# Cross-attention and routed experts on one core: a third pair of stacks, four stored copies for both batches, a loop body of six steps

## The chip, the cores and the metric

One NeuronCore of a Trainium2 chip runs the whole program; the other cores are idle. The metric is the device time of one launch in microseconds (us), less is better. Engines are named as in the profile: PE (TensorE), DVE (VectorE), ACT (ScalarE), POOL (GpSimd), SP (SyncE, which only issues DMAs). A name with q, such as SPq, is the engine's sequencer.

## The reference, cut to what matters

```python
# x, ctx: (128 batches, 128 tokens, 256)
q = layernorm(x) @ Wq.T;  k = ctx @ Wk.T;  v = ctx @ Wv.T
# q, k: 32 sub-heads of 8 dims; v: 16 heads of 16 dims
att = softmax(q @ k.T / sqrt(8))               # per sub-head, 128 x 128
att = att[:, :, 0] - lam * att[:, :, 1]        # pairs of sub-heads
x = x + att @ v
h = layernorm(x)
top2 of sigmoid(h @ gate_w.T) over 16 experts, weights normed, times 2.5
x = x + sum over the 2 experts of w_e * (silu(h @ w_gate_e) * (h @ w_up_e)) @ w_down_e
      + (silu(h @ ws_gate) * (h @ ws_up)) @ ws_down
```

## The kernel before

**Steps.** The 128 batches go in pairs: 64 attention steps, each with two batches (u = 0, 1) of 128 tokens. Every engine runs the same software pipeline: while step `it` has its scores, softmax and output made (stage c), step it+1 (stage b) has its values and its row maxima made, step it+3 (stage a) its projections, it-1 and it-2 the second layer norm and the routing. After the steps, 144 tiles of 128 gathered rows go through the experts.

**Stacks.** The scores of a sub-head have only 8 contraction dims. So q and k are split into three bf16 parts each, and six products of parts (q0k0, q1k1, q2k0, q0k1, q1k0, q0k2) are stacked along the contraction dim: 48 rows. Two halves h of 16 sub-heads each sit at partitions 0 and 64. To get from tokens of features into this layout, the parts are written to `stack_dram` (`put_parts`, L349) and read back as rows (`load_stacks`, L358) into `q_st` and `k_st`, two bf16 tiles of 8 KB a partition for each of two parities. Before, each of the six copies of each operand is written once: 12 DMAs of 128 KB a step, and 8 DMAs of 192 KB read them back, one for each of q and k, u and h.

**Maxima.** `maxima` (L490) multiplies the first 48 rows to get the scores by query, DVE reduces them (`reduce_max`, L982), PE turns the maxima (L543), ACT copies them (`copy_max`, L798) and SP writes them as two more rows of `q_st` (`put_max`, L365), so that `scores` (L483, 50 rows) gives scores less the row's maximum. Slot k of a step's 16 has 4 score matmuls and 4 matmuls of maxima of the next step; `both` (L497) holds their waits: `d_stk` at k = 0, 4, 8, 12 for the maxima's stacks, `d_m` at k = 0 and 8 for the maxima's rows of the scores.

**SP's order.** SP's `step` (L384) is written out by hand: what stands behind a waiting DMA waits too. The two halves u of a stack are loaded at different times, since with two parities a buffer comes free by halves.

**Loop.** `steps` (L308) gives each engine steps -4 to 3 as straight code, then a hardware loop (`Fori`, L302) whose body is two steps, run 27 times, then steps 58 to 66 as straight code. In the loop, waits compare with a register (L282, L294).

Of the kernel before, what the change touches and what calls it, by code (L numbers as in the profile page):

```python
# [22 lines left out]
P = 128  # L23
# [3 lines left out]
COPIES = 6  # L27
Q_COPIES, K_COPIES = (0, 1, 2, 0, 1, 0), (0, 1, 0, 1, 0, 2)
# [15 lines left out]
class Step:  # L44
# [11 lines left out]
    def par(self):  # L56
        return self.off % 2

# [9 lines left out]
def program(nc, x, ctxT, lq1, lk1, lq2, lk2, wqT, wkT, wvT, gate_wT, w_gu, w_dn, ws_gu, ws_dn, out):  # L68
# [25 lines left out]
    stack_dram = nc.dram_tensor("stack_dram", (2, 2, 2, 2, COPIES, HALF, SHH, P), BF16, kind="Internal").ap()  # L94
# [5 lines left out]
    with ExitStack() as st:  # L100
# [34 lines left out]
        def stack(n):  # L135
            return stacks.bitcast(BF16)[:, n * SHH * SW:(n + 1) * SHH * SW].rearrange("p (u j t) -> p u j t", u=2, j=SHH)

        q_st, k_st = [stack(0), stack(2)], [stack(1), stack(3)]
# [85 lines left out]
        d_stk = [[sem(f"d_stk{u}{h}") for h in range(2)] for u in range(2)]  # L224
# [36 lines left out]
        STK = 2 * 16  # L261
# [8 lines left out]
        first, lo, hi, end = -4, 4, NS - 6, NS + 3  # L270
        PAD_STEPS = (*range(lo), *range(hi, hi + 4))
# [36 lines left out]
        def steps(eng, body):  # L308
            pipeline(eng, body, first, lo, hi, end, 2)
# [28 lines left out]
        def _(sp):  # L338
# [10 lines left out]
            def put_parts(s, n, part, landed, copies, at):  # L349

                for u in range(2):
                    for h in range(2):
                        wait(sp, d_stk[u][h], STK, s, -STK)
                for i in at:
                    sp.dma_start(stack_dram[s.par(), n, :, :, i].rearrange("h u d j t -> (d j) (h u) t"),
                                 part[:, copies[i], :].rearrange("p (v t) -> p v t", t=P)).then_inc(landed, 16)

            def load_stacks(s, u, h):  # L358

                p = s.par()  # L360
                for n, buf in ((0, q_st[p]), (1, k_st[p])):
                    sp.dma_start(buf[64 * h:64 * h + ROWS, u, :, :].rearrange("p j t -> p (j t)"),
                                 stack_dram[p, n, h, u].rearrange("r d j t -> (r d) (j t)")).then_inc(d_stk[u][h], 16)

            def put_max(s, u):  # L365

                wait(sp, a_mT, 2, s, u + 1)
                for h in range(2):
                    row = 64 * h + ROWS
                    sp.dma_start(q_st[s.par()][row:row + 2, u, :, :],  # L370
                                 mxT[u][2 * SHH * h:2 * SHH * (h + 1), :]).then_inc(d_m[u], 16)
# [12 lines left out]
            def step(it):  # L384
# [6 lines left out]
                if b.is_in(0, NS):  # L391
                    wait(sp, p_st, NCH, it)
                    wait(sp, p_mx, NCH, b)
                    load_stacks(b, 1, 1)
                    load_stacks(b, 1, 0)
                if n2.is_in(0, NS):
                    wait(sp, g_qs, 1, n2, 1)
                    put_parts(n2, 0, qp, d_qw, Q_COPIES, range(PARTS))
                if it.is_in(0, NS):
                    put_max(it, 1)  # L400
                if n2.is_in(0, NS):
                    put_parts(n2, 0, qp, d_qw, Q_COPIES, range(PARTS, COPIES))
                    wait(sp, g_ks, 1, n2, 1)
                    put_parts(n2, 1, kp, d_kw, K_COPIES, range(COPIES))
# [4 lines left out]
                if n2.is_in(0, NS):  # L409
                    wait(sp, p_st, NCH, it, NCH // 2)  # L410
                    wait(sp, p_mx, NCH, b, NCH // 2)
                    wait(sp, d_qw, PW_Q, n2, PW_Q)
                    wait(sp, d_kw, PW_K, n2, PW_K)
                    if n2.k is None and n2.off < 2:
                        sp.wait_ge(g_ones, n2.off + 1)
                    load_stacks(n2, 0, 1)
                if b.is_in(0, NS):
                    put_max(b, 0)
                if n2.is_in(0, NS):
                    load_stacks(n2, 0, 0)  # L420
                if b.is_in(0, NS):
                    wait(sp, g_x2, 4, it, 0)
                    sp.dma_start(x_res[1 - p][:, :, :],
# [1045 lines left out]
```

## Time and profile before

| | |
|---|---|
| median of three timed runs | 2260.15 us (2256.93 to 2262.98) |
| the profiled execution, its own time | 2249.22 us |
| its span, first to last instruction | 2247.5 us |
| PE, DVE, ACT, POOL busy | 90%, 71%, 63%, 64% of the span |
| granted PE clock, mean | 0.972 |
| DMA packets | 616,921, of them 447,811 under 512 B |

The span divides into a start (0 to 65 us), 64 steps (65 to about 1675 us) and the experts' tiles. Busy shares are averages over these; what a change is worth must be read in the stretch that it touches, from what ends the waits there. PE rows have modelled ends, so a gap of PE is to be read from the starts of its groups.

### The profile page before, as it was taken

What the parts mean: (1) busy time and instruction counts of PE and PEld (TensorE: products, weight loads), DVE (VectorE), ACT (ScalarE), POOL (GpSimd) and SP (SyncE); (2) the same over time, 40 slices, a digit from 0 to 9 for tenths busy, and PEclk for the clock granted to TensorE, in tenths of its full rate; (3) what the DMA queues carried; (4) which work ended last, traced back from release to release, by engine and by line L of the source; (5) the groups of instructions that cost most, each with busy time, mean ns of one, the idle gap of its engine ahead of it and who ended that gap; (6) DMA issues with size and microseconds to landing.
All of it is one profiled execution on the core that took longest, in us unless ns stands there. A gap on an engine that the chain in (4) does not pass through costs nothing.

```text
span 2247.5 us, 76469 instructions
## 1 busy us (share of the span) xinstructions
PE 2021.7 (90%) x20840; PEld 1405.2 (63%) x20840; DVE 1584.5 (71%) x4623; ACT 1426.2 (63%) x3511; POOL 1446.2 (64%) x2183
## 2 busy tenths in 40 slices
PE   4999999999999999999999999999977988889996
PEld 3666665566656566656656566666546877768775
DVE  3777777777777777778777777778765655546554
ACT  2777777777777777777776777777763444434443
POOL 4466777767677676767676767767664555545554
PEclk8899999999999999999999999999987999999999
DMA  5997777777777777777777777878846777667774
GB/s 133 222 225 192 187 195 190 178 189 184 191 190 184 186 194 185 185 183 182 191 193 178 184 188 190 194 181 216 228 173 180 223 214 214 199 178 220 220 223 127
DMA packets 616921, 432.05 MB, mean 192 GB/s; under 512 B 447811, under 2 KB 562634, under 8 KB 616400
## 3 DMA queue, kind: packets, MB, share of 16 engines
q1 hardware_dynamic: 556528, 319.91, 58.3%
q0 software_dynamic: 32256, 84.47, 11.8%
q10 hardware_dynamic: 28000, 26.03, 3.8%
q8 instruction: 64, 1.05, 0.2%
q14 instruction: 73, 0.60, 0.1%
HBM read 234.59 MB, written 197.72 MB: 192 GB/s over the span
## 4 chain that ended last, share of the span: by engine, by line
PE 67%; DVE 15%; issue 10%; ACT 3%; DMA 2%; SPq 1%; POOL 1%; DVEq 1%; another core or an unknown queue 1%; ACTq 0%; POOLq 0%
PE mx_ps L494 11%; PE o_ps L527 7%; DVE mx L982 6%; PE ms_ps L778 5%; PE o_ps L538 5%; PE ms_ps L555 5%; PE mx_ps L557 4%; PE mx_ps L555 4%; PE ms_ps L576 4%; PE st_ps L756 3%; PE mx_ps L556 3%; PE ms_ps L583 3%; PE st_ps L487 3%; PE ms_ps L556 3%; PE ms_ps L557 2%
## 5 line engine op out<-in xcount | busy, mean ns | idle before, releaser
L982 DVE TENSOR_REDUCE mx<-mx_ps 128x4 f32<-128x512 f32 x1024 | 686.3, 685 | 300.4 <-PE mx_ps L494 294.2
L826 ACT ACTIVATE prob<-st_ps 128x512 f32<-128x512 f32 x1024 | 604.5, 598 | 357.8 <-PE st_ps L487 353.5
L494 PE MATMUL mx_ps<-stacks 48*128 48x128 bf16 x4096 | 396.7, 221 | 67.6 <-DVE mx L982 33.8
L487 PE MATMUL st_ps<-stacks 50*128 50x128 bf16 x4096 | 394.9, 220 | 0.0
L494 PEld LDWEIGHTS mx_ps<-stacks 48*128 48x128 bf16 x4096 | 230.9, 95 | 228.6 <-issue 105.9
L527 PE MATMUL o_ps<-prob,v_sb 128*32 128x256 f32 x4096 | 331.6, 396 | 0.8 <-ACT prob L826 0.4
L1344 POOL DMA_INDIRECT rows_dram<-rowt,posi x256 | 253.7, 991 | 67.6 <-issue 64.3
L555 PE MATMUL ms_ps<-e_lo 128*128 128x256 f32 x768 | 264.7, 345 | 18.1 <-issue 11.1
L923 ACT ACTIVATE rows_T<-st_ps 128x256 fp32r<-128x256 f32 x288 | 111.7, 388 | 192.2 <-PE st_ps L756 137.3
L487 PEld LDWEIGHTS st_ps<-stacks 50*128 50x128 bf16 x4096 | 229.8, 95 | 2.5 <-issue 1.5
L1413 POOL DMA_INDIRECT sums_dram<-stacks x144 | 141.7, 984 | 130.4 <-DVE stacks L1220 70.2
L1417 POOL DMA_INDIRECT out<-stacks x144 | 141.7, 984 | 121.7 <-issue 62.6
L556 PE MATMUL ms_ps<-e_lo 128*128 128x256 f32 x768 | 219.7, 286 | 0.0
L557 PE MATMUL ms_ps<-e_lo 128*128 128x256 f32 x768 | 219.2, 285 | 0.0
L555 PE MATMUL mx_ps<-e_hi,rows_T 128*128 x576 | 192.3, 334 | 27.7 <-DVE prob L1213 25.6
L555 PEld LDWEIGHTS ms_ps<-e_lo 128*128 128x128 f32 x768 | 147.6, 192 | 97.2 <-issue 69.9
L1207 DVE TENSOR_TENSOR rows_lo<-st_ps,rows_T 128x256 fp32r<-128x256 f32 x288 | 121.1, 421 | 95.5 <-issue 51.1
L1220 DVE SCALAR_TENSOR_TENSOR stacks<-ms_ps,stacks 128x256 f32<-128x256 f32 x288 | 138.6, 481 | 67.2 <-PE ms_ps L778 49.0
L778 PE MATMUL ms_ps<-w_dn_sb,v_sb 128*128 x576 | 176.3, 388 | 1.0 <-DVE stacks L1220 0.4
L1350 POOL DMA_INDIRECT base_dram<-base_t,posi x128 | 139.1, 1087 | 53.1 <-issue 47.9
L538 PE MATMUL o_ps<-ident,oT 128*128 128x128 f32 x1024 | 169.6, 289 | 0.4 <-issue 0.4
L557 PE MATMUL mx_ps<-e_hi,rows_lo 128*128 x576 | 165.0, 286 | 0.0
(155 smaller groups left out, 4694.4 us busy)
## 6 DMA issues: line engine op xcount, KB each, us to landing
stack_dram<-w_dn_sb SPq DMA_DIRECT2D x768, 128.0 KB
stacks<-stack_dram SPq DMA_DIRECT2D x512, 192.0 KB
stacks<-rows_dram SPq DMA_DIRECT2D x288, 130.0 KB
w_dn_sb<-in_x SPq DMA_DIRECT2D x64, 256.0 KB
w_dn_sb<-in_ctxT SPq DMA_DIRECT2D x64, 256.0 KB
x_res<-in_x SPq DMA_DIRECT2D x64, 256.0 KB
stacks<-sums_dram SPq DMA_DIRECT2D x78, 128.0 KB
stacks<-base_dram SPq DMA_DIRECT2D x76, 128.0 KB
```

The lines of the kernel that those rows point to most:

```text
L487: return pe.matmul(st_ps[k % 2][:, i * P:(i + 1) * P], k_st[p][64 * h:64 * h + KROWS, u, j, :], q_st[p][64 * h:64 * h + KROWS, u, j, :], s ...
L494: return pe.matmul(mx_ps[k % 2][:, i * P:(i + 1) * P], q_st[p][64 * h:64 * h + ROWS, u, j, :], k_st[p][64 * h:64 * h + ROWS, u, j, :], sta ...
L527: mm = pe.matmul(OT[SLOT * g:SLOT * (g + 1), gg * SW:(gg + 1) * SW], v_sb[s.par()][:, (u * HEADS + 2 * c + i) * SLOT:(u * HEADS + 2 * c + ...
L538: mm = pe.transpose(out_ps, src, ident[:, :])
L555: pe.matmul(out_ps, rnd(still[0]), rnd(moving[0]), start=start, stop=False)
L556: pe.matmul(out_ps, rnd(still[0]), rnd(moving[1]), start=False, stop=False)
L557: return pe.matmul(out_ps, rnd(still[1]), rnd(moving[0]), start=False, stop=stop)
L778: pe.matmul(eo_ps[t.off % 2][:, 0:D], hid_T[t.off % 4][:, :], w_dn_sb[:, bass.ds(down, 1), :].rearrange("p e n -> p (e n)"), start=True, s ...
L826: nc.scalar.activation(prob[k % 4][:, :], st_ps[k % 2][:, :], ACT.Exp, scale=float(HALF) ** -0.5).then_inc(a_exp, 1)
L982: v.tensor_reduce(mx[:, u, c * CHUNK:(c + 1) * CHUNK], mx_ps[k % 2][:, :].rearrange("p (c n) -> p c n", c=CHUNK), AX.X, ALU.max).then_inc( ...
L1344: g.indirect_dma_start(rows_dram[k][:, :], bass.IndirectOffsetOnAxis(ap=posi[p][:, u, k:k + 1], axis=0), rowt[p][:, u, :], None).then_inc( ...
L1413: g.indirect_dma_start(sums_dram[:, :], bass.IndirectOffsetOnAxis(ap=row[:, C_NEXT:C_NEXT + 1], axis=0), sums, None, bounds_check=N_FIRST ...
```

## The change

- `COPIES` goes from 6 to 4. `stack_dram` has one row for both batches (512 B runs instead of 256 B), and the parts are written with 8 DMAs of 128 KB a step instead of 12. The stored order is q parts (0, 1, 2, 0) and k parts (2, 0, 0, 1); the load reads all four and then two of them again (from copy 0 for q, from copy 2 for k), which gives the same six products.
- `load_stacks` brings both batches at once, with 8 DMAs: for q, then k, the 32 rows of four copies and the 16 rows of two, each for h = 1 and then h = 0. The tile's layout has u inside.
- A third pair of stacks lies in the last 16 KB a partition of `e_hi`, which nothing else uses until the last steps. A step's stack is its number modulo 3. POOL sets three key tiles to -1 at the start instead of two.
- The loop's body becomes six steps (2 and 3 both divide it), run 9 times.
- `d_stk` becomes one semaphore for each h and parity; PE waits for it at k = 0 and k = 4 only.
- SP's step: all loads of step it+2 come after its own puts and the context's load, then x's load, then the maxima's rows of step it+1 for u = 0, then the residual.

```diff
-COPIES = 6
-Q_COPIES, K_COPIES = (0, 1, 2, 0, 1, 0), (0, 1, 0, 1, 0, 2)
+COPIES = 4
+Q_COPIES, K_COPIES = (0, 1, 2, 0), (2, 0, 0, 1)
+Q_AGAIN, K_AGAIN = 0, 2
...
-    stack_dram = nc.dram_tensor("stack_dram", (2, 2, 2, 2, COPIES, HALF, SHH, P), BF16, kind="Internal").ap()
+    stack_dram = nc.dram_tensor("stack_dram", (2, 2, 2, COPIES, HALF, SHH, SW), BF16, kind="Internal").ap()
...
+        def stack_of_experts(n):
+            whole = e_hi[:, :, :, :].rearrange("p e k n -> p (e k n)").bitcast(BF16)
+            return whole[:, (2 + n) * SHH * SW:(3 + n) * SHH * SW].rearrange("p (j w) -> p j w", j=SHH)
+
+        q_st, k_st = [stack(2), stack_of_experts(0), stack(0)], [stack(3), stack_of_experts(1), stack(1)]
...
-            pipeline(eng, body, first, lo, hi, end, 2)
+            pipeline(eng, body, first, lo, hi, end, 6)
...
+            def load_stacks(s):
+
+                p, i = s.par(), s.third()
+                for n, buf, again in ((0, q_st[i], Q_AGAIN), (1, k_st[i], K_AGAIN)):
+                    for row, copy, m in ((0, 0, COPIES), (COPIES * HALF, again, 2)):
+                        for h in (1, 0):
+                            sp.dma_start(buf[64 * h + row:64 * h + row + m * HALF, :, :].rearrange("p j w -> p (j w)"),
+                                         stack_dram[p, n, h, copy:copy + m].rearrange("r d j w -> (r d) (j w)"),
+                                         max_dma_last_dim=4096).then_inc(d_stk[h][p], 16)
...
-                if b.is_in(0, NS):
-                    wait(sp, p_st, NCH, it)
-                    wait(sp, p_mx, NCH, b)
-                    load_stacks(b, 1, 1)
-                    load_stacks(b, 1, 0)
...
                 if n2.is_in(0, NS):
-                    wait(sp, p_st, NCH, it, NCH // 2)
-                    wait(sp, p_mx, NCH, b, NCH // 2)
+                    wait(sp, p_st, NCH, it)
+                    wait(sp, p_mx, NCH, it)
                     wait(sp, d_qw, PW_Q, n2, PW_Q)
                     wait(sp, d_kw, PW_K, n2, PW_K)
...
-                    load_stacks(n2, 0, 1)
...
+                    load_stacks(n2)
...
-                    if k % 4 == 0:
-                        wait(pe, d_stk[u][1 - k // 4 % 2], STK, b, STK)
+                    if k in (0, 4):
+                        wait_par(pe, d_stk[1 - k // 4], STK, b)
...
-            for i in range(2):
-                g.memset(k_st[i][:, :, :, :], -1.0).then_inc(g_ones, 1)
+            for i in range(3):
+                g.memset(k_st[i][:, :, :], -1.0).then_inc(g_ones, 1)
```

SP's DMAs in one whole step (step 3, the last ahead of the loop), before. `stack_dram<-w_dn_sb` are the puts of the parts, `stacks<-stack_dram` the loads, `stacks<-mxT1` and `stacks<-mxT0` the maxima's rows of u = 1 and u = 0.

```order
L362 DMA stacks<-stack_dram 48x2048 x4
L355 DMA stack_dram<-w_dn_sb 128x4x128 x3
L370 DMA stacks<-mxT1 2x16x128 x2
L355 DMA stack_dram<-w_dn_sb 128x4x128 x9
L407 DMA w_dn_sb<-in_ctxT 128x512
L362 DMA stacks<-stack_dram 48x2048 x2
L370 DMA stacks<-mxT0 2x16x128 x2
L362 DMA stacks<-stack_dram 48x2048 x2
L423 DMA x_res0<-in_x 128x2x256
L427 DMA w_dn_sb<-in_x 128x2x256
```

The same step now; `e_hi` is the third pair of stacks.

```order
L363 DMA stack_dram<-w_dn_sb 128x2x256 x4
L381 DMA stacks<-mxT1 2x16x128 x2
L363 DMA stack_dram<-w_dn_sb 128x2x256 x4
L412 DMA w_dn_sb<-in_ctxT 128x512
L372 DMA stacks<-stack_dram 32x2x2048 x2
L372 DMA stacks<-stack_dram 16x2x2048 x2
L372 DMA stacks<-stack_dram 32x2x2048 x2
L372 DMA stacks<-stack_dram 16x2x2048 x2
L424 DMA w_dn_sb<-in_x 128x2x256
L381 DMA e_hi<-mxT0 2x16x128 x2
L429 DMA x_res0<-in_x 128x2x256
```

The maxima's rows of u = 0 had two loads ahead of them since the puts; they now have eight and the load of x.

At the start, before: the first stacks, from the puts of step 0 to those of step 1.

```order
L355 DMA stack_dram<-w_dn_sb 128x4x128 x12
L407 DMA w_dn_sb<-in_ctxT 128x512
L362 DMA stacks<-stack_dram 48x2048 x4
L427 DMA w_dn_sb<-in_x 128x2x256
L362 DMA stacks<-stack_dram 48x2048 x4
```

And now:

```order
L363 DMA stack_dram<-w_dn_sb 128x2x256 x8
L412 DMA w_dn_sb<-in_ctxT 128x512
L372 DMA stacks<-stack_dram 32x2x2048 x2
L372 DMA stacks<-stack_dram 16x2x2048 x2
L372 DMA stacks<-stack_dram 32x2x2048 x2
L372 DMA stacks<-stack_dram 16x2x2048 x2
L424 DMA w_dn_sb<-in_x 128x2x256
```

The first maxima needed the first two of the loads; they now need the seventh of eight.

## Rows read from the trace of the kernel before

**Rows 1.** The page: span, busy time, DMA share in 40 slices.

```profile
span 2247.5 us, 76469 instructions
PE 2021.7 (90%) x20840; PEld 1405.2 (63%) x20840; DVE 1584.5 (71%) x4623; ACT 1426.2 (63%) x3511; POOL 1446.2 (64%) x2183
DMA  5997777777777777777777777878846777667774
```

**Rows 2.** Windows: two steps in the loop, two steps behind it (length, busy, clock, DMA).

```profile
1302.50:1353.20 50.70, 47.08 (x553) 30.60 (x552) 39.38 (x117) 36.93 (x84) 35.92 (x59) 1.00 0.75 188
1531.60:1580.90 49.30, 46.88 (x553) 30.68 (x552) 39.17 (x117) 37.33 (x84) 36.63 (x59) 1.00 0.96 241
```

**Rows 3.** Line 494, 158 to 1550 us: what PE's idle time there waited for.

```profile
  DVE mx L982: 105.5, 260
  issue: 104.5, 427
```

**Rows 4.** Line 302, the loop's end: PE's sequencer, ns min/median/max.

```profile
L302 PEldq COMPARE_BRANCH  x27: 76/208/243, 205.4 to 1530.3; - x27
```

**Rows 5.** DMA queue of PE's instructions, 100 to 204 us, then 210 to 1530 us.

```profile
q8 instruction: 10, 0.16, 0.7%
q8 instruction: 1, 0.02, 0.0%
```

**Rows 6.** DMA issues: the smallest load of the start (KB each, us to landing).

```profile
gw_sb<-in_gate_wT SPq DMA_DIRECT2D x1, 16.0 KB, 4.0
```

**Rows 7.** PE's timeline at a loop's end, the branch at 814.5 us.

```profile
815.15 0.66 PE L538 MATMUL o_ps<-ident,oT 128*128 128x128 f32 x4
815.74 0.23 PE L494 MATMUL mx_ps<-stacks 48*128 48x128 bf16 x1
```

**Rows 8.** Windows: a step at the lower clock, and the next one.

```profile
841.30:867.90 26.60, 24.90 (x277) 15.99 (x278) 19.77 (x59) 18.61 (x43) 17.90 (x30) 0.94 0.74 179
867.90:893.40 25.50, 23.60 (x277) 15.33 (x276) 19.71 (x58) 18.47 (x43) 17.97 (x30) 1.00 0.76 187
```

**Rows 9.** Timelines of the step from 765.1 to 790.56 us: POOL, SP, ACT, PE.

```profile
775.46 1.16 POOL L1313 TENSOR_TENSOR w_dn_sb<-k_rest,w_dn_sb 128x512 bf16<-128x512 f32 x1 [0.68 <-ACT w_dn_sb L849]
776.98 3.22 SPq L355 DMA_DIRECT2D stack_dram<-w_dn_sb  x6
780.57 0.36 SPq L407 DMA_DIRECT2D w_dn_sb<-in_ctxT  x1
782.07 0.80 SPq L362 DMA_DIRECT2D stacks<-stack_dram  x2
784.18 1.31 SPq L370 DMA_DIRECT2D stacks<-mxT  x2
783.84 0.26 ACT L798 ACTIVATE mxT<-o_ps 64x128 bf16<-64x128 bf16 x1
790.56 0.23 PE L494 MATMUL mx_ps<-stacks 48*128 48x128 bf16 x1
```

**Rows 10.** The chain of waits at the start (start us, us, what).

```profile
40.18 4.00 DMA stacks<-stack_dram
78.14 3.38 DMA stack_dram<-w_dn_sb
83.12 3.80 DMA stacks<-mxT
```

**Rows 11.** SP's DMA queue: 765.1 to 769.1, 763.5 to 765.1, 778.2 to 781.2 us.

```profile
q1 hardware_dynamic: 256, 0.78, 86.9%
q1 hardware_dynamic: 502, 0.49, 94.7%
q1 hardware_dynamic: 2588, 0.64, 96.7%
```

**Rows 12.** POOL's timeline at the start.

```profile
3.70 6.96 POOL L1261 MEMSET stacks<- 128x4096 bf16 x2
16.23 0.22 POOL L1283 TENSOR_SCALAR ve<-mv 128x2 f32<-128x2 f32 x1 [4.05 <-DVE mv L1013]
```

More of the change, by code:

```diff
@@ L57, in par, with third @@
         return self.off % 2
+    def third(self):
+        return self.off % 3
     def pair(self):
@@ L135, in stack @@
         def stack(n):
-            return stacks.bitcast(BF16)[:, n * SHH * SW:(n + 1) * SHH * SW].rearrange("p (u j t) -> p u j t", u=2, j=SHH)
-        q_st, k_st = [stack(0), stack(2)], [stack(1), stack(3)]
+            return stacks.bitcast(BF16)[:, n * SHH * SW:(n + 1) * SHH * SW].rearrange("p (j w) -> p j w", j=SHH)
+        def stack_of_experts(n):
+            whole = e_hi[:, :, :, :].rearrange("p e k n -> p (e k n)").bitcast(BF16)
+            return whole[:, (2 + n) * SHH * SW:(3 + n) * SHH * SW].rearrange("p (j w) -> p j w", j=SHH)
+        q_st, k_st = [stack(2), stack_of_experts(0), stack(0)], [stack(3), stack_of_experts(1), stack(1)]
         prob = [sb(f"prob{i}", [P, 512]) for i in range(4)]
@@ L223, in program @@
         d_qw, d_kw = sem("d_qw"), sem("d_kw")
-        d_stk = [[sem(f"d_stk{u}{h}") for h in range(2)] for u in range(2)]
+        d_stk = [[sem(f"d_stk{i}{h}") for i in range(2)] for h in range(2)]
         d_m = [sem(f"d_m{i}") for i in range(2)]
@@ L260, in program @@
         PW_Q, PW_K = COPIES * 16, COPIES * 16
-        STK = 2 * 16
+        STK = 4 * 16
         MR = 2 * 16
@@ L270, in program @@
         first, lo, hi, end = -4, 4, NS - 6, NS + 3
+        assert (hi - lo) % 6 == 0 and (NS - 1) % 3 == 0
         PAD_STEPS = (*range(lo), *range(hi, hi + 4))
@@ L347, in _, with put_parts @@
                 sp.dma_start(lam_in[:, n, :], src.partition_broadcast(P)).then_inc(d_w, 16)
[L349 to L363, printed above, removed]
+            def put_parts(s, n, part, landed, copies):
+                for h in range(2):
+                    wait_par(sp, d_stk[h], STK, s.plus(-2))
+                for i, r in enumerate(copies):
+                    sp.dma_start(stack_dram[s.par(), n, :, i].rearrange("h d j w -> (d j) h w"),
+                                 part[:, r, :].rearrange("p (h w) -> p h w", h=2)).then_inc(landed, 16)
+            def load_stacks(s):
[6 more added lines that the diff above has]
+                                         max_dma_last_dim=4096).then_inc(d_stk[h][p], 16)
             def put_max(s, u):
@@ L369, in put_max @@
                     row = 64 * h + ROWS
-                    sp.dma_start(q_st[s.par()][row:row + 2, u, :, :],
+                    sp.dma_start(q_st[s.third()][row:row + 2, :, u * P:(u + 1) * P],
                                  mxT[u][2 * SHH * h:2 * SHH * (h + 1), :]).then_inc(d_m[u], 16)
@@ L401, in step @@
                 if n2.is_in(0, NS):
-                    put_parts(n2, 0, qp, d_qw, Q_COPIES, range(PARTS, COPIES))
                     wait(sp, g_ks, 1, n2, 1)
-                    put_parts(n2, 1, kp, d_kw, K_COPIES, range(COPIES))
+                    put_parts(n2, 1, kp, d_kw, K_COPIES)
                 if xs.is_in(1, NS):
@@ L428, in step @@
                                  x_g[bass.ds(xs.plus(1).idx(), 1)].rearrange("g p u d -> (g p) u d")).then_inc(d_x, 16)
+                if b.is_in(0, NS):
+                    put_max(b, 0)
+                    wait(sp, g_x2, 4, it, 0)
+                    sp.dma_start(x_res[1 - p][:, :, :],
+                                 x_g[bass.ds(b.idx(), 1)].rearrange("g p u d -> (g p) u d")).then_inc(d_res[1 - p], 16)
             steps(sp, step)
```

24 lines of the change are left out of this document (8 added, 16 removed).

## The prediction

> **What bounds the kernel now.** I read the page first, then windows of whole steps, then what PE's idle time waited for, then SP's timeline against the deadline that PE sets, and last the chain of waits at the start.
>
> The page has PE busy for 90% of a span of 2247.5 us; DMA is busy too, at seven to nine tenths [rows 1]. So the first question is whether DMA bounds anything. In the loop it doesn't. Two steps in the loop take 50.7 us, 25.35 each, at a DMA share of 0.75; two whole steps behind the loop, with the same 553 matmuls, take 49.3 us, 24.65 each, at a DMA share of 0.96 [rows 2]. More DMA, shorter steps. And line 494, where PE waits for the stacks and for the maxima's rows, sat idle for DVE (105.5 us) and for issue (104.5 us), with no line for a DMA [rows 3]. A step in the loop is a chain of PE, DVE and ACT.
>
> At the start it is otherwise. The chain of waits goes through the puts (3.38 us to land), the loads (4.00 us) and the maxima's rows (3.80 us) [rows 10], in the slices where the DMA share is nine tenths [rows 1]. That holds for steps 0 to 2 only; then PE's own work is longer.
>
> **The change part by part.** The sum is made against the profiled execution, 2249.2 us; the median of the timed runs, 2260.15, is 10.9 above it, and I add that at the end.
>
> *Fewer loop ends.* The loop's branch is taken 26 times now and 8 times after. One costs PE's sequencer 0.208 us [rows 4]: 18 x 0.208 = 3.7, say -4 us.
>
> *A longer body.* This is the term that I expect to decide. In straight code PE fetches ten blocks of 16 KB in 104 us, some 2.4 a step of 25 us; in the loop, from 210 to 1530 us, it fetches one [rows 5]. A body of two steps, five blocks, is held and isn't fetched again. A body of six steps is some 15 blocks. No row shows what the engine does with that. If it isn't held, each of the 8 taken branches goes to code that must come first. Bounds: 0, if it is held; 4.0 us, what the 16 KB load takes from issue to landing [rows 6]. PE has work queued when it branches at 814.5: it starts the next step's first group at 815.74 [rows 7], so about 1.0 us is covered. I take the far end, 4.0 - 1.0 = 3.0 us, x 8 = +24 us, because the nearest rows for code not held are those in straight code, where each block is fetched as it is reached. ACT, DVE and POOL have bodies three times as long too, and stall beside PE, not behind it: they wait for PE a third of the time.
>
> The Trainium skill (Runtime: NRT & Kernel Launch, Instruction fetch mechanics) gives TensorE an instruction memory of 128 KiB and the others 32 KiB, filled in blocks of 16 KiB, and says that a taken branch out of it must wait for the fetch. Rows 5 agree with it as far as they go: 80 KB was held. By that rule a body of some 240 KB stalls at each branch.
>
> *The clock.* A step in which the granted clock fell to 0.94 on average (a stretch at 1.2 instead of 2.4 GHz) took 26.6 us, the next 25.5 [rows 8]. A stall of 3 us may bring that on. Bounds 0 and 8 times 1.1; half, +4 us.
>
> *The puts.* Before, 12 x 512 = 6,144 packets of 256 B a step, 17.9 ns each (3.0 us x 16 x 0.967 / 2,588) [rows 11], its third row: 6.9 us of all 16 DMA engines. After, 2,048 packets of 512 B. Their price isn't in the trace; it lies between 17.9 ns and the 48 ns of a 1 KB packet (1.6 x 16 x 0.947 / 502) [rows 11], its second row, so 2.3 to 6.1 us; middle 4.2, 2.7 us less a step. In the loop this is hidden already (rows 2), and worth nothing. It counts at the start.
>
> *The loads and the maxima's rows, in the loop.* PE needs both the maxima's rows and all of the next stack's h = 1 at the next step's first group, 790.56 in the step shown [rows 9]. Before, the parts of k are ready at 776.62, six puts are issued to 780.20, the loads 1.87 us behind them at 782.07, the maxima's rows from 784.18 to 785.49. After: four puts, to 779.13; loads from 781.0; eight at 0.43 us to 784.4; x's load, 0.4; the maxima's rows, ready on ACT at 784.1, from 784.8 to 786.1. As issued, only 0.6 us later. But they stand behind 1.57 MB of stacks and 0.26 MB of x in one queue. The rows give two rates: 0.78 MB in 4.0 us, 195 GB/s, for loads beside POOL's scatters, and 0.49 MB in 1.6 us, 306 GB/s, for x [rows 11]. Two loads (0.39 MB) landed in 4.00 us [rows 10], 2 us more than their transfer, so the last row lands at 781.0 + 2 + 1.83 / rate: 789.0 at the better rate, 1.6 us early, and 792.4 at the worse, 1.8 us late. The middle falls on the deadline. I take 0, since the loads of both halves now alternate and fewer put packets stand in the way; the bad end is 1.8 x 58 steps = 104 us.
>
> *At the start.* The same order sits on the chain. In steps 0 to 2: two puts less, -1.1 us; six loads and x ahead of the maxima's rows, +3.0 us of issue; 1.44 MB more ahead in the queue, of which 3.0 us of issue drain about half at 250 GB/s, +2.8 us; less 2.7 for the puts: +2.0, x 3 = 6. For the very first stack, two puts less, seven loads instead of two to wait for: -1.1 + 2.2, and 1.0 MB more less what the issue drains, +1.8: 3. Together +9 us. POOL's third tile costs 3.5 us (6.96 / 2) ahead of an idle time of 4.05 [rows 12]: nothing.
>
> *Where the waits that go were.* PE's waits at k = 8 and 12 had long been met. The third pair of stacks removes SP's wait for the middle of a step; with six puts still running then, it wasn't what was late.
>
> Sum: -4 + 24 + 4 + 0 + 9 = +33. 2249.2 + 33 = 2282 profiled, 2293 as a median.
>
> **The rivals.**
>
> *The maxima's rows come late in every step* (25%). For it: the deadline is met by about nothing at the middle rate. Against: x's packets ran at 306 GB/s in the same queue, and the puts that come ahead are fewer. At 1.0 us a step, 58 more: 2351. The Trainium skill (SBUF — State Buffer, Can I just issue two DMAs to hit both halves?) says that loads at partitions 0 and 64 in flight together gain only 6%, since one transfer's span picks its ports. By that rule the alternating halves bring nothing, and the time is this rival's; the 195 GB/s of rows 11, for loads of one half after the other, don't contradict it.
>
> *The long body costs nothing* (15%). If the body is held, or its head is fetched ahead, the 24 and the 4 go: +5, 2265.
>
> *The loop's steps come down to the pace of the steps behind it* (18%), the other side: faster. The mechanism would be PE's idle time ahead of line 494 in the loop: the queue is less full, SP is less often late, two of PE's register waits a step go. Price: 0.7 us x 54 = 38 us [rows 2], so 33 - 38 without the stalls' 28, -33: 2227. It decides the sign only from 0.6 us a step if the stalls come, 0.1 if not. Against: rows 2, where DMA was busier in the faster steps, and rows 3, where the idle time is DVE's and issue's, which keep all their register waits.
>
> **How the numbers follow.** The forecast has 42%, the others 25, 15 and 18. Its own range is 2268 to 2312: stalls of 1 to 4 us at each branch, 0 to 15 us at the start. The range for 8 in 10 leaves out half of the faster case below 2225, and the worse part of the late rows above 2360. About 0.3%, 7 us, is what a measurement can tell from no change. Faster by more: 0.18. Within: most of the free long body and a little of the forecast, 0.14. Slower: 0.68.
>
> **What would show it.** Right: PE's instruction queue has some 15 packets of 16 KB for each of 9 passes, some 130 more than now; PE is idle by 2 to 3 us ahead of the first group behind each of 8 branches, 152 us apart; other steps in the loop stay at 25.2 to 25.5 us; the start is about 9 us longer. The late rows would show as idle time of line 494's group for the DMA of the maxima's rows in most steps, and the chain of waits going through them. The free body: no instruction packets in the loop, or many but no idle time at the branches. I am wrong on the other side if steps inside the body come under 24.9 us.

## The result, and the profile after

The changed kernel takes 2472.82 us (median of 4 runs, 2455.72 to 2483.22), the kernel before 2258.93 us on the same chip (4 runs, 2256.93 to 2262.98): a ratio of 1.0937, 95% interval 1.0871 to 1.1003. It is slower, as forecast, by 214 us where +33 was forecast, and outside the range.

Two more measurements of it gave 1.0866 (1.0792 to 1.0939) and 1.0966 (1.0904 to 1.1029). The kernels of the experiments ran on four chips: on two of them the kernel before takes 2259 and 2249 us, on the other two 2062 us. Each is compared with the kernel before on its own chip, by ratio. The changed kernel itself was not run on a chip of the 2062 us kind.

The page of the changed kernel, for [rows 1], with the chain's shares and the two queues of instructions:

```profile
span 2481.4 us, 74118 instructions
PE 2101.6 (85%) x20840; PEld 1476.5 (60%) x20840; DVE 1590.1 (64%) x4623; ACT 1449.1 (58%) x3511; POOL 1451.3 (58%) x2184
PEclk7888989899999889989899899898998899999999
DMA  4765555566655556665556566555673676757674
q8 instruction: 201, 3.29, 0.6%
q14 instruction: 273, 2.24, 0.4%
PE 46%; DMA 20%; SPq 13%; issue 9%; POOL 4%; DVE 3%; ACT 2%; another core or an unknown queue 2%; ACTq 0%; POOLq 0%; DVEq 0%
```

PE's busy share fell from 90 to 85%, and DMA is busy for five or six tenths where it was seven: over the whole span nothing is full. The time is waiting, and a fifth of the chain that ended last goes through transfers.

Windows (length, PE, PEld, DVE, ACT, POOL busy, clock, DMA share, GB/s): the first steps of before and of after, then three steps of after in the loop, the third with a loop end. They answer to [rows 2] and [rows 8].

```profile
65.40:158.10 92.70, 88.80 (x1065) 57.71 (x1066) 70.91 (x184) 71.90 (x157) 51.34 (x88) 0.95 0.96 231
```

```profile
72.70:186.60 113.90, 93.64 (x1045) 60.95 (x1046) 70.17 (x181) 72.71 (x156) 53.06 (x90) 0.87 0.66 170
449.90:478.50 28.60, 25.00 (x273) 16.52 (x274) 18.94 (x57) 18.30 (x41) 17.21 (x29) 0.91 0.57 142
478.50:507.20 28.70, 26.08 (x277) 17.02 (x277) 19.89 (x59) 18.86 (x41) 17.09 (x28) 0.88 0.56 139
507.20:538.30 31.10, 23.76 (x277) 15.53 (x278) 19.67 (x58) 18.60 (x41) 20.52 (x33) 0.93 0.63 153
```

Where the 233.9 us between the two profiled spans went (a step runs here from its first exponential on ACT to the next step's):

| part | before | after | difference |
|---|---|---|---|
| up to the first step | 65.4 | 72.7 | +7.3 |
| steps 0 to 3 | 92.7 | 113.9 | +21.2 |
| steps 4 to 57, mean x 54 | 25.47 | 28.96 | +188.5 |
| steps 58 to 62, mean x 5 | 23.91 | 26.96 | +15.3 |
| rest | | | +1.6 |

So 225 of 234 us are in the 63 steps, spread over all of them, with more in the first four (5.3 us each, against 3.5 and 3.1). What PE waited for at line 496 (494 before), whole span, for [rows 3]:

```profile
  issue: 297.9, 422
  DMA stacks<-mxT: 154.8, 51
  DVE mx L984: 99.0, 260
  DMA e_hi<-mxT: 33.1, 11
```

The maxima's rows (`mxT`), which had no line in [rows 3], are named 62 times in 63 steps. SP's timeline of the step from 478.5 to 507.2 us (start, us, issues), then PE at its end and the chain of waits, for [rows 9]:

```profile
491.00 1.96 SPq L363 DMA_DIRECT2D stack_dram<-w_dn_sb  x4
493.82 0.35 SPq L412 DMA_DIRECT2D w_dn_sb<-in_ctxT  x1
494.67 4.11 SPq L372 DMA_DIRECT2D e_hi<-stack_dram  x8
499.12 0.40 SPq L424 DMA_DIRECT2D w_dn_sb<-in_x  x1
499.71 1.34 SPq L381 DMA_DIRECT2D stacks<-mxT  x2
506.78 0.21 PE L496 MATMUL mx_ps<-e_hi 48*128 48x128 bf16 x1 [1.75 <-DMA stacks<-mxT]
```

```profile
500.43 6.21 DMA stacks<-mxT
```

The second of the two transfers of 8 KB takes 6.21 us from its issue. In that time the queue is busy with loads. SP's queue over the load stretch of this step (packets, MB, share of 16 engines):

```profile
q1 hardware_dynamic: 653, 1.80, 92.0%
```

That is 1.80 MB in 9.0 us (495.1 to 504.1), 200 GB/s, of the loads and of the packets behind them. SP's queue alone keeps the 16 DMA engines 92.0% busy in this stretch: here, unlike over the whole step, they are all but full.

A picture of the usual step comes from the single packets of the trace. The maxima's rows are SP's only packets of 256 B now, the stacks' loads the only ones of 4 KB; of those there are 384 a step in both kernels, so what is new is that they come in one go. Medians over steps 6 to 55, in us from the step's start; the version is described in the next section where it isn't one of the two:

| version | rows issued | first packet | last packet | next step starts |
|---|---|---|---|---|
| before | 17.1 | 18.1 | 19.2 | 25.3 |
| after | 20.3 | 26.1 | 27.2 | 28.5 |
| after, third run | 20.2 | 25.9 | 26.9 | 28.2 |
| x behind the rows | 19.1 | 24.0 | 25.0 | 27.0 |
| rows in ACT's queue | 16.9 | 22.7 | 24.6 | 26.8 |
| one half at a time | 20.7 | 28.2 | 29.2 | 30.6 |
| more bytes, to DRAM | 22.9 | 26.3 | 27.2 | 28.8 |
| rows between the halves | 17.4 | 20.8 | 21.8 | 24.4 |
| the same, no loop | 16.1 | 17.9 | 19.2 | 24.3 |

In after the loads are first issued at 15.6, their first packet starts at 16.7 and the last ends at 25.6; the rows' packets end at 27.2, and 1.3 us later the next step begins (0.8 us to PE's first matmul, the rest to the exponential). Where the rows end by 22, the step no longer depends on them. The third run, the one with more bytes, and the one without a loop are from the chip where the kernel before takes 2249 us; the other four from the chips with 2062 us.

### The profile page after: what moved, and what is told of

The parts are those of the page before. It is cut to its first block, busy times and chain, and to the rows that moved or that the text cites. A ratio compares the mean times of both kernels' runs of the same rounds, so it can differ in the third digit from the quotient of the medians.

```text
span 2481.4 us, 74118 instructions
## 1 busy us (share of the span) xinstructions
PE 2101.6 (85%) x20840; PEld 1476.5 (60%) x20840; DVE 1590.1 (64%) x4623; ACT 1449.1 (58%) x3511; POOL 1451.3 (58%) x2184
## 4 chain that ended last, share of the span: by engine, by line
PE 46%; DMA 20%; SPq 13%; issue 9%; POOL 4%; DVE 3%; ACT 2%; another core or an unknown queue 2%; ACTq 0%; POOLq 0%; DVEq 0%
DMA stacks<-mxT 9%; SPq L372 8%; PE mx_ps L496 6%; PE o_ps L529 5%; PE ms_ps L780 5%; DMA e_hi<-mxT 4%; PE ms_ps L578 4%; PE mx_ps L559 3%; PE mx_ps L557 3%; PE ms_ps L557 3%; DMA stack_dram<-w_dn_sb 3%; PE st_ps L758 3%; PE mx_ps L558 3%; PE ms_ps L551 2%; PE ms_ps L585 2%
## 5 line engine op out<-in xcount | busy, mean ns | idle before, releaser
L984 DVE TENSOR_REDUCE mx<-mx_ps 128x4 f32<-128x512 f32 x1024 | 692.0, 686 | 529.5 <-PE mx_ps L496 423.3
L496 PE MATMUL mx_ps<-stacks 48*128 48x128 bf16 x2752 | 281.0, 230 | 179.1 <-issue 63.1
L529 PE MATMUL o_ps<-prob,v_sb 128*32 128x256 f32 x4096 | 351.4, 417 | 1.0 <-ACT prob L828 0.4
L496 PEld LDWEIGHTS mx_ps<-stacks 48*128 48x128 bf16 x2752 | 163.8, 98 | 292.1 <-issue 173.8
L557 PE MATMUL ms_ps<-e_lo 128*128 128x256 f32 x768 | 290.5, 378 | 19.5 <-issue 10.8
L1346 POOL DMA_INDIRECT rows_dram<-rowt,posi x256 | 253.7, 991 | 67.6 <-issue 65.4
L489 PE MATMUL st_ps<-stacks 50*128 50x128 bf16 x2752 | 279.8, 228 | 0.8 <-ACT prob L828 0.8
L558 PE MATMUL ms_ps<-e_lo 128*128 128x256 f32 x768 | 240.2, 313 | 0.0
L557 PEld LDWEIGHTS ms_ps<-e_lo 128*128 128x128 f32 x768 | 167.2, 218 | 121.6 <-issue 97.8
L559 PE MATMUL ms_ps<-e_lo 128*128 128x256 f32 x768 | 238.6, 311 | 0.0
L1285 POOL TENSOR_SCALAR ve<-mv 128x2 f32<-128x2 f32 x128 | 28.8, 225 | 280.9 <-DVE mv L1023 141.9
L496 PE MATMUL mx_ps<-e_hi 48*128 48x128 bf16 x1344 | 137.5, 229 | 64.2 <-DMA stacks<-mxT 50.0
L558 PEld LDWEIGHTS ms_ps<-e_lo 128*128 128x128 f32 x768 | 171.3, 223 | 1.5
L559 PEld LDWEIGHTS ms_ps<-e_lo 128*128 128x128 f32 x768 | 170.3, 222 | 0.0
```

What stands on the lines that cost most here:

```text
L489: return pe.matmul(st_ps[k % 2][:, i * P:(i + 1) * P], k_st[p][64 * h:64 * h + KROWS, j, u * P:(u + 1) * P], q_st[p][64 * h:64 * h + KROWS ...
L496: return pe.matmul(mx_ps[k % 2][:, i * P:(i + 1) * P], q_st[p][64 * h:64 * h + ROWS, j, u * P:(u + 1) * P], k_st[p][64 * h:64 * h + ROWS, ...
L529: mm = pe.matmul(OT[SLOT * g:SLOT * (g + 1), gg * SW:(gg + 1) * SW], v_sb[s.par()][:, (u * HEADS + 2 * c + i) * SLOT:(u * HEADS + 2 * c + ...
L557: pe.matmul(out_ps, rnd(still[0]), rnd(moving[0]), start=start, stop=False)
L558: pe.matmul(out_ps, rnd(still[0]), rnd(moving[1]), start=False, stop=False)
L559: return pe.matmul(out_ps, rnd(still[1]), rnd(moving[0]), start=False, stop=stop)
```

## The experiments

**First group: body length, queue, order, hint.** All four ran where the kernel before takes 2061.98 us; the times in their expectations were reckoned from 2260.

`before_six`: the kernel before with the changed kernel's body length alone.

```
-            pipeline(eng, body, first, lo, hi, end, 2)
+            pipeline(eng, body, first, lo, hi, end, 6)
```

> The kernel before with a loop body of six steps instead of two, nothing else. Theory of the body (the 8 taken branches stall, 5 to 9 us each as PE's branch records in the changed kernel show, less some 1 us of queued work): 2259 - 4 + 8 x 5 = about 2295 us. Rival, the whole loss is SP's order and the branches only look long because PE waits there anyway: 2252 to 2262 us.

2115.8 us, ratio 1.025 (1.0232 to 1.0268): +54 us. The theory's 2295 us is a ratio of 1.016, the rival's at most 1.001: the long body costs by itself, and more than was expected. The loop's branch on PE's sequencer (ns, min/median/max), for [rows 4], and three steps, of which the first holds a loop end:

```profile
L302 PEldq COMPARE_BRANCH  x9: 83/4632/5930, 296.3 to 1495.2; - x9
```

```profile
423.40:451.70 28.30, 23.52 (x277) 15.60 (x277) 19.62 (x59) 18.79 (x43) 21.45 (x35) 0.95 0.74 183
451.70:477.20 25.50, 24.88 (x277) 16.32 (x277) 19.80 (x59) 18.85 (x41) 14.33 (x25) 0.92 0.75 178
477.20:501.20 24.00, 23.42 (x278) 15.48 (x279) 19.79 (x59) 18.67 (x43) 17.91 (x30) 1.00 0.76 183
```

The branch of the long body takes 4.6 us instead of 0.208. The step with it is 4.3 us longer than a plain one and the next, at a clock of 0.92, 1.5 us longer: 5.8 x 8 = 46 of the 54 us.

`after_hint`: the changed kernel's loop is told that it will be branched back (`hint_back_edge=True`).

> The changed kernel with the loops' ends told to the instruction fetch ahead (a prefetch hint at each body's head), nothing else. Theory of the body (code that is fetched only when the branch is taken): the branch records of 5 to 9 us go back to under 1 us, 8 x 5 = 40 us less: about 2433 us. Rival, the branches only wait for what is late anyway: 2465 to 2480 us, no change.

2373.23 us, ratio 1.1498 (1.1462 to 1.1533). The branch still takes a median of 5.4 us, so the expectation of under 1 us fell, and the steps inside the body take 28.4 us as in the changed kernel, which was timed only on chips of the other kind. If the hint saves anything at the branches, it isn't what the kernel lost. I use this version as the nearest stand-in for the changed kernel on this chip.

`after_max_act`: the first batch's maxima's rows are issued by ACT, into a queue of its own, as soon as they are computed.

```
-                    put_max(b, 0)      (SyncE)
+                        wait(act, a_mT, 2, b, 1)
+                        for h in range(2):
+                            act.dma_start(q_st[b.third()][row:row + 2, :, 0:P], ...)
```

> The changed kernel, with the maxima's rows of u = 0 issued on ACT's queue right after ACT has made them, so that they no longer stand behind eight loads and x's load in SP's queue; ACT pays two more issues a step. Theory of the queue (these rows come 3 us late in each of some 60 steps, and the stall brings the low clock): steps back to 25.5 us, 2473 - 60 x 2.8 = about 2305 us. Rival, the stacks themselves come late (the loads take 8.7 us for 1.57 MB and end 3 us ahead of the late start of the next step): at least 2400 us, and PE then waits for stacks<-stack_dram.

2294.65 us, ratio 1.1145 (1.1093 to 1.1197). The theory's 2305 us is a ratio of 1.02, and the rival's 2400 us one of 1.06, so the theory's time fell. The rival's reason didn't hold either: from 158 to 1600 us the matmuls and weight loads of the maxima's line waited for the rows (`mxT`) 56 times and for the stacks (`stack_dram`) 7 times. The rows are issued 3.3 us earlier than in the changed kernel, and their first packet still comes 5.8 us after the issue, as there. What holds them back is not SyncE's order alone: in another queue they wait as long, while the DMA engines are full of loads.

`after_split` and `after_split_2`: the loads of half 1, then the maxima's rows, then the loads of half 0, x and x_res.

```
-                    load_stacks(n2)
+                    load_stacks(n2, (1,))
+                if b.is_in(0, NS):
+                    put_max(b, 0)
+                if n2.is_in(0, NS):
+                    load_stacks(n2, (0,))
```

> The changed kernel with SP's order split: the four loads of h = 1, the maxima's rows of u = 0, the four loads of h = 0, x. Theory of the queue: 0.79 MB ahead of the rows instead of 1.83 MB, so they land at 21 to 23 us of the step instead of 27, and steps are 25.5 to 26 us: 2300 to 2340 us. Rival, stacks late by themselves: little gain, at least 2400 us.

> The split version (half 1's loads, maxima's rows of the first batch, half 0's loads, x), once more beside the other three so that all are read against one set of runs of the kernel before. Volume theory: normal steps no longer than before the change, only loop ends longer: ratio 1.02 to 1.055, and clearly below the version with x behind. Rival (moving the rows alone isn't it): ratio over 1.07.

2174.51 us, ratio 1.0545 (1.0524 to 1.0565), and 2171.51 us, 1.0522 (1.0504 to 1.0539). Against the stand-in's 2373 us, moving the rows alone took off 199 us, of a loss of 311. It is less than was expected: 2300 to 2340 us were ratios of 1.02 to 1.035. Two thirds of the plain steps inside the body are back at 23.7 to 24.2 us, those of `before_six`; the rest take about 25. What stays long is the step with a loop end, 30 to 35 us, and the next by 1 to 2 us. So with the rows on time the long body is left with 112 us here, twice the 54 of `before_six`.

**Second group**, on a chip where the kernel before takes 2259.23 us.

`after_again`, and later `after_third`: the changed kernel, unaltered.

> The changed kernel itself, unaltered, on the chip of the other runs, where the kernel before takes 2062 us. It gives the reference that the single edits are to be read against. If the back-edge hint of an earlier run did nothing, it takes what that run took, 2373 us (ratio 1.15); if the ratio of the first measurement carries over, 2255 us (1.094). The two theories on its steps: by the queue theory (the maxima's rows stand behind all eight loads and x) steps inside a body take some 28 us against 23.7 in the split version; by the body theory alone they would take 23.7 and only every sixth would be long.

> The changed kernel itself, unaltered, beside the next three, so that the single edits made on a chip where the kernel before takes 2062 us can be read against it, should this be such a chip. Volume theory: ratio to the kernel before 1.14 to 1.16 there (the version with a branch hint took 1.15), with x ahead of the rows worth 0.03 to 0.05 of it and the alternating halves saving 0.07 to 0.09; 1.08 to 1.10 on a chip where the kernel before takes 2259 us.

2463.93 and 2466.21 us, ratios 1.0866 and 1.0966. Neither ran on the chip that was hoped for. The ratio of the first measurement carried over to chips of its kind; the median step takes 28.1 and 28.2 us.

`before_max_last`: the kernel before, the rows behind the first batch's four loads, x_res and x.

> The kernel before, in which the maxima's rows of the first batch are issued behind the last loads, x_res and x, as in the changed kernel, and nothing else is changed. Queue theory: these rows then come late in each step, +1.5 to +4 us a step, 2150 to 2300 us in all. Rival (the new form of the loads, 4 KB packets and 1.57 MB in one go, is what makes them late): up to 20 us slower, 2062 to 2082 us.

2292.88 us, ratio 1.0123 (1.0058 to 1.0188): +34 us, between the two expectations, nearer to the rival's. The first packet comes at 21.5 us and the last at 22.3, the step stays at 25.4. So the place in the order costs 3 us, which the old kernel mostly had to spare in the loop; there the changed kernel needs the second batch's 0.79 MB ahead of the rows to get to 27. At the start there is nothing to spare: steps 0 to 3 take 111.9 us, against 92.7 before and 113.9 after. That is 19 of the 43 us between the two profiled spans.

`before_straight` and `before_straight_2`: no hardware loop, the 54 middle steps written out.

```
-            with eng.Fori(0, (hi - lo) // unroll) as k:
-                for off in range(unroll):
-                    body(Step(k, lo + off, unroll))
+            for it in range(lo, hi):
+                body(Step(None, it))
```

> The kernel before with its 54 middle steps written out in a row, without a hardware loop. Body theory: what the six-step body costs (+54 us) is a stall at each taken branch, and nothing else of long code costs time: so without branches the time is that of the kernel before or a little less, 2040 to 2062 us (of the +54, none stays). Rival (long code itself costs: instructions are fetched late all along): at least as slow as the six-step body, 2116 us or more.

> The kernel before with its middle steps written out, once more, to see if what it gains holds on another chip. Body theory (a taken branch of the two-step body costs 1.4 us on every second step, and straight code is fetched ahead at no cost): ratio 0.96 to 0.98 on a chip with 2259 us, 0.97 to 1.00 on one with 2062 us, where steps inside a six-step body take 23.7 us.

2192.59 us, ratio 0.969 (0.962 to 0.9761), and 2181.3 us, 0.9692 (0.9652 to 0.9731). By ratio this is the fastest version, faster than both kernels. The first expectation had 0.99 to 1.00; it was right that straight code doesn't cost, and had not seen that the short loop does. Two steps of the second run:

```profile
448.10:472.30 24.20, 23.28 (x280) 15.38 (x276) 19.50 (x59) 18.62 (x41) 18.03 (x30) 1.00 0.81 203
472.30:496.60 24.30, 23.63 (x283) 15.38 (x276) 19.52 (x59) 18.62 (x41) 18.03 (x30) 1.00 0.79 196
```

24.3 us instead of 25.35 [rows 2]. From 210 to 1530 us PE fetches 130 packets of instructions here, against 1 in [rows 5], and the median step of this part, 24.3 us, shows nothing of it.

`after_split_straight` and `after_split_straight_2`: both edits, on the changed kernel.

> The changed kernel with the maxima's rows of the first batch between the two halves' loads, and with its 54 middle steps written out in a row. Two causes theory (queue position and the branch of the long body explain all): 2174 us less nine loop ends at some 12.5 us above a normal step = 2062 us, the kernel before's time, within 15. Rival (four copies with 4 KB packets, or the third pair in the experts' room, cost or gain by themselves): outside 2045 to 2080 us.

> The split version of the changed kernel with its middle steps written out, once more, beside the same version of the kernel before. Two causes theory (bytes ahead of the maxima's rows, and the branches of the long body, explain the whole difference): the same as before_straight_2 within 0.5%. Rival (the new layout costs or gains by itself): more than 1% apart.

2203.77 us, ratio 0.9721 (0.9654 to 0.9788), and 2188.9 us, 0.971 (0.9664 to 0.9756), steps of 24.3 us. The expectation of 1.00 was met in what it argued (the loss goes with the two causes) and missed in that straight code gains 3% besides. Beside the same version of the kernel before, on the same two chips, it is 0.3 to 0.5% slower, within the intervals. Nothing that can be measured is left of the loss, so the new layout, the third pair and the new puts neither cost nor gain.

**Third group**, on a chip where the kernel before takes 2061.63 us.

`after_straight`: the changed kernel without a loop, its SyncE order kept.

> The changed kernel with its 54 middle steps written out in a row, the SyncE order as changed. The changed kernel is 1.087 to 1.094 times the kernel before. Additive theory: the loop ends (nine, some 4 us above a normal step) go and the late maxima's rows stay, steps of some 28 us: ratio 1.06 to 1.08. Rival (what makes the rows late is knocked-on delay from the loop ends, which never heals): steps fall to 24.4 us as in the split version without a loop, ratio 0.97 to 1.00.

2272.8 us, ratio 1.101 (1.0984 to 1.1035): steps of 27.1 us. The absence of every loop end does not heal the steps, so the late rows are no after-effect of the stalls. (1.06 to 1.08 was expected; that had been taken from the other chip, where the kernel before has slower steps to be compared with.) But the loop ends are not all that went: beside the stand-in with its loop, 28.4 us a step, this is 100 us less in all, and the plain steps too are 1.3 us shorter. Their loads are first issued at 14.3 us instead of 15.6.

`after_x_behind`: the rows directly behind the loads, ahead of x.

> The changed kernel with the maxima's rows of the first batch directly behind the eight loads, ahead of x instead of behind it. Volume theory (1.57 MB of loads in one go stand ahead of the rows, in the transfer engines as well as in SyncE's order): the rows come at most 1.5 us earlier, ratio to the kernel before 1.05 to 1.09. Rival (x is what delays the rows): as good as the split version, ratio under 1.05.

2275.39 us, ratio 1.1026 (1.0975 to 1.1077). The rows' packets end at 25.0 instead of about 27, the step takes 27.0. x was worth 1.2 to 1.5 us a step; the loads are the larger part. The ratio is a little above the 1.05 to 1.09 of the theory and far from the rival's 1.05.

`after_even`: the alternation undone.

```
-                for n, buf, again in (...):
-                    for row, copy, m in (...):
-                        for h in (1, 0):
+                for h in (1, 0):
+                    for n, buf, again in (...):
+                        for row, copy, m in (...):
```

> The changed kernel with the alternation of the head halves undone: the four loads of half 1, then the four of half 0, everything else as changed. If two halves in flight at once bring nothing: the changed kernel's ratio, 1.07 to 1.10. If the alternation speeds the loads up: slower than the changed kernel by over 1%, ratio over 1.10.

2532.14 us, ratio 1.2279 (1.2258 to 1.2299), the slowest of all: the alternating halves speed the loads up. SP's queue over one load stretch of this version (10.6 us, 486.9 to 497.5), beside the 9.0 us of the changed kernel above:

```profile
q1 hardware_dynamic: 619, 1.67, 92.7%
```

158 GB/s instead of 200 in these two stretches. Over steps 6 to 55 the mean 4 KB packet took 369 ns instead of 305 (308 in `after_x_behind`, on the same chip), from the first packet of the loads to the end of their last there are 10.6 us instead of 8.8, and the rows end at 29.2 us. So the gain is about a fifth.

**Fourth group**, on a chip where the kernel before takes 2248.97 us.

`after_more`: four more transfers of 0.13 MB in the loads, from the stored copies to a spare place in DRAM.

> The changed kernel with four more transfers of 0.13 MB each among the loads of a step (a part of the stored copies, to a spare place in DRAM): 2.10 MB instead of 1.57 MB between the puts and the maxima's rows, all else unchanged. Volume theory: the 384 packets of 4 KB take some 8.7 us a step now, so a third more is +2.9 us on each of 60 steps, +175 us on the changed kernel (+0.08 in ratio). Rival (the steps are long for the rows' place in SyncE's order or for the wait on x, not for the bytes ahead): the four issues alone, 4 x 0.45 us = +1.8 us at most and mostly hidden, under +60 us.

2482.36 us, ratio 1.1044 (1.0991 to 1.1097), +16 us on `after_third` where the bytes' count said +175. SP's timeline of one step and PE at its end:

```profile
469.32 1.75 SPq L373 DMA_DIRECT2D stacks<-stack_dram  x4
471.11 1.19 SPq L377 DMA_DIRECT2D spare_dram<-stack_dram  x2
472.35 1.98 SPq L373 DMA_DIRECT2D stacks<-stack_dram  x4
474.37 1.11 SPq L377 DMA_DIRECT2D spare_dram<-stack_dram  x2
475.84 1.21 SPq L429 DMA_DIRECT2D w_dn_sb<-in_x  x1
477.24 1.42 SPq L386 DMA_DIRECT2D stacks<-mxT  x2
481.94 0.28 PE L501 MATMUL mx_ps<-stacks 48*128 48x128 bf16 x1 [3.34 <-DMA stacks<-mxT]
```

My expectation fell; the rival's "under +60 us" was met, though its first reason wasn't: the rows now stand four transfers further back. The rows are issued 2.8 us later than in the changed kernel, and their last packet is only 0.3 us later: the step doesn't follow the issue. Nor does it follow the count of bytes: a third more 4 KB packets went through, at a mean of 261 ns instead of 305. If the loads' packets took as long as without them, the 128 added ones took 127 ns each (512 x 261 less 384 x 306; an estimate). My reading is that the rows wait for the loads on their way into the stacks, and packets to DRAM fit in between those; no run separates the two kinds of packet.

## Why the prediction was wrong

**The step that failed** is "The middle falls on the deadline. I take 0", for the loads and the maxima's rows in the loop. It cost about 3 us on every step, some 190 us (199 on the chip of `after_split`, by moving the rows alone). The prediction had the mechanism, named it as the rival with 25%, and priced it at 1.0 us a step; even its bad end, 1.8 us, was too little. What went into it:

- *The rate.* I set the 195 GB/s of loads against the 306 GB/s of x [rows 11] and took the middle. The first row was for the same packets to the same place; the loads and x ran at 200. From the loads' first issue to the end of the rows the sum has 11.4 us at its worse end (792.4 - 781.0), and the table has 11.6 (27.2 - 15.6). "The worse" end of the bounds was the forecast.
- *When the loads start.* This comes on top of the bad end. The step that [rows 9] show begins by the table's measure, the first exponential, at 767.66:

```profile
767.66 0.60 ACT L826 ACTIVATE prob<-st_ps 128x512 f32<-128x512 f32 x1 [2.00 <-PE st_ps L487]
```

  So "loads from 781.0" is 13.3 us into it, and in after they are issued at 15.6. The sum kept the old times of the parts; they come later when the head of the step is slow (see the clock, below) and, by `after_straight`, in the long loop. The rows, "only 0.6 us later" as issued, were issued 3.2 us later (20.3 against 17.1).
- *What follows the landing.* Between the rows' last packet and the next step's first exponential lie 1.3 us in after, `after_straight` and `after_more` and 1.4 in `after_even` (1.8 and 2.2 by the table where the rows came a little earlier, with x behind and from ACT's queue). 15.6 + 11.6 + 1.3 = 28.5, the step that was measured. By the same count the bad end is 13.3 + 11.4 + 1.3 = 26.0, so most of what is missing is the loads' later start. The sum compared the landing with a matmul's start and left the 1.3 us out; that cost it little, since the exponential that follows the group of 790.56 came only at 792.30.
- *No relief from the halves.* I argued the choice of 0 by the alternation. It is real, larger than I thought, and already in the 200 GB/s; without it the step takes 30.6 (`after_even`).

**The Trainium skill's rule** (SBUF — State Buffer, "Can I just issue two DMAs to hit both halves?"), by which two transfers to both halves gain 6%, stood for the rival. The measurement differs from it: 305 against 369 ns a packet and 8.8 against 10.6 us for the loads, about a fifth, with four transfers of each half issued in turn. The rival came true for another reason. By the rule the alternation would be worth 6% of 10.6 us, 0.6 us a step or some 40 us (an estimate); it changed 2532 into some 2373 us.

**The longer body.** "4.0 - 1.0 = 3.0 us, x 8 = +24": right in kind, too small. The branch on PE in the changed kernel, and its timeline behind the branch at 529.5 us:

```profile
L311 PEldq COMPARE_BRANCH  x9: 83/7174/9038, 354.4 to 1745.8; - x9
```

```profile
537.58 0.28 PE L496 MATMUL mx_ps<-stacks 48*128 48x128 bf16 x1 [6.76 <-issue]
```

7.2 us instead of 4.0, and 6.8 us of idle time. Part of that covers the wait for the rows, so the step grows by some 4.5 us over its neighbours: 36 us for 8. That is not all that the long body costs: on the 2062 us kind of chip, writing the steps out took 100 us off (`after_straight` against the stand-in), and with the rows on time the long body is left with 112 us (`after_split`). The instruction packets came as foreseen: 201 against some 130 more than 64. The size that I had was one load's landing at an idle start; that in the loop the fetch is slower because it shares the engines with the loads and the scatters is likely, and not tested. The Trainium skill (Runtime: NRT & Kernel Launch, Instruction fetch mechanics) says that a taken branch whose target isn't in the current window of two pages must wait for the fetch. The stalls agree, 4.6 us in `before_six` and 7.2 in after, and so does their absence in straight code; the width does not, since on PE a body of some five such blocks was held [rows 5].

**Fewer loop ends.** "18 x 0.208 = -4" was too small by a factor of seven or more. On this kind of chip the short loop's ends are not 0.2 us: steps alternate between 24.65 and 26.05 us, which gives 1.4 x 18 = 25 us, and written out they all take 24.3, which gives 67 us for 26 ends, or 46 for 18. The sequencer's record is not what a loop end costs. [Rows 2] showed 0.7 us a step of it; I put that down to nothing. So by these profiles the change saved 36 us or more of short ends and paid 36 or more for its own eight. Whether the two cancel on this kind of chip is open, since neither `before_six` nor `after_split` ran there. On the other kind they don't: `before_six` costs 54 us net.

**The start.** "Together +9": measured +7.3 up to the first step and +21.2 in steps 0 to 3. The chain of waits there, for [rows 10]:

```profile
39.69 7.58 DMA stacks<-stack_dram
64.53 7.41 DMA stacks<-mxT
91.25 7.39 DMA e_hi<-mxT
```

7.6 us for the loads instead of 4.00, and 7.4 for the rows instead of 3.80. The cause is the same: with the rows between the halves' loads, the part up to the first step is back at 65.2 to 67.1 us and steps 0 to 3 at 92.9 to 94.5 (four runs of the split versions), and moving the rows back in the old kernel alone made 111.9 of its 92.7. "That holds for steps 0 to 2 only" was an error of its own: it held for all of them.

**The clock.** "+4" was too small as well. In steps 4 to 57 of before the granted clock fell to half in 6 stretches, 20 us in all; in after in 49 stretches, 276 us. PE waits for the rows at the end of each step, and the clock falls about when it starts again (0.88 to 0.91 in the windows above). Steps of one run with and without a stretch at the lower clock, in its first 14 us, show what goes with it: 27.3 us (40 steps) against 25.4 (10) in `after_straight`, 27.6 (27) against 26.0 (23) in `after_x_behind`. In the longer ones the fifth exponential comes at 8.4 us instead of 6.9, and the loads are issued at 14.7 instead of 12.9, and at 15.8 instead of 14.1. So late rows, the lower clock, late loads and late rows again form a circle, and the sum had priced its parts apart. This is a comparison of steps, not an experiment: no run sets the clock alone, and in after itself only 5 of 50 steps were free of it.

**Right** were that the puts are worth nothing in the loop, that the third pair frees no time, and that no rows stood for the faster case: no step came under 24.9 us in the changed kernel's body. The sign was right as well, but mostly by luck: of 234 us some 190 come from the term that I put at 0, and the one that was to decide, +24 for the long body, met savings that I had at 4 and that were 25 or more.

## What to carry to other kernels

A small transfer that the next stage waits for should not be issued behind the stage's bulk loads: here it came only when their packets had gone, in their queue or in another (5.8 us from issue to first packet in both). When two rows give a rate, take the one with the same packet and the same destination, add what lies between the last packet and the first instruction, and measure all of it from one mark in the step, before calling something on time.

A loop body longer than what was seen to be held costs several microseconds at each taken branch, while long code in a row cost nothing that showed here; compare the steps inside a loop with those outside it before pricing a branch by its own record.

## What the runs showed of the hardware that was not expected

- Loads to partitions 0 to 47 and 64 to 111, alternating one by one, moved at 200 GB/s (305 ns a packet of 4 KB); the same loads half by half at 158 (369 ns). In the kernel before, which loads two of one half and then two of the other, the mean was 274 ns.
- 4 KB packets to DRAM among loads to SBUF raised the rate of the whole: 512 packets at 261 ns took the place of 384 at 305.
- Steps that neither the rows nor a loop end holds take 23.7 us on one kind of chip and 24.3 on the other (`after_split` inside its body, `after_split_straight`), with the kernel before at 2062 and 2259 us. Where transfers set the step, both gave 28.1 to 28.5. More of the difference lies behind the steps: from the start of step 63 to the end, 503 to 506 us against 587 to 618 over all versions. What the chips differ in stays open.
- The stall at the long body's branch is longer in every version of the changed kernel (medians from 5.4 us in `after_hint` over 7.2 in after and 8.5 in `after_split` to 9.4 in `after_even`) than in the old layout (4.6), at nearly the same number of instruction packets (194 to 201). Why was not tried.
